# First attention: the rotation of q on VectorE, moved from between the maxima of slots 14 and 15 to ahead of the maximum of slot 14, behind the residual

## What is computed

```python
qkv = jnp.einsum('bsd,ed->bse', x, w_qkv)          # x: 32 x 256 x 128
q, k, v = jnp.split(qkv, 3, axis=-1)               # 16 heads of 8
q = _apply_rope(q, cos_emb, sin_emb)
k = _apply_rope(k, cos_emb, sin_emb)
scores = jnp.einsum('bhqd,bhkd->bhqk', q, k) / jnp.sqrt(8)
attn = jax.nn.softmax(scores, axis=-1)
out = jnp.einsum('bhqk,bhkd->bhqd', attn, v)
...
x = _layernorm(x + out @ w_out.T + b_out)
...
```

## Time and profile before

| | |
|---|---|
| median of 3 runs | 1514.56 us |
| lowest and highest run | 1513.92, 1516.4 us |
| profiled execution, its own time | 1516.91 us |
| profiled execution, span from first to last instruction | 1514.7 us |
| of the span: PE, PEld, DVE, ACT, POOL busy | 96%, 75%, 78%, 70%, 64% |
| loop of the first attention | about 60 to 460 us, 14.52 us a step |

### The profile page before, as it was taken

The page is one execution under the profiler, slowest core; times in us unless marked ns, Lnnn a source line. Parts: engine busy times, 40 slices in busy tenths (PEclk is TensorE's granted clock), DMA queues, the critical chain, the costliest instruction groups (busy, mean ns, idle before and its releaser), DMA issues. The chain is left out here.

```text
span 1514.7 us, 55309 instructions
## 1 busy us (share of the span) xinstructions
PE 1453.8 (96%) x17642; PEld 1143.0 (75%) x17642; DVE 1181.1 (78%) x3338; ACT 1057.0 (70%) x2581; POOL 966.3 (64%) x1160
## 2 busy tenths in 40 slices
PE   6999999999999899979999999999999999998998
PEld 4455555555554699959899999989998999997997
DVE  5788888888889388878778787878887888864666
ACT  2577777778778788847677777777777777773332
POOL 5555656656562277777777787788778877852222
PEclk9799999999999999979999999999999999999999
DMA  5454454545544001222322222222222222201111
GB/s 143 130 140 135 140 140 129 140 129 140 143 128 111 22 32 34 74 68 71 91 69 70 90 77 80 70 88 79 80 70 84 81 79 70 82 17 35 62 62 52
DMA packets 174124, 133.93 MB, mean 88 GB/s; under 512 B 13787, under 2 KB 145126, under 8 KB 174054
## 3 DMA queue, kind: packets, MB, share of 16 engines
q1 hardware_dynamic: 172512, 132.18, 30.0%
q10 hardware_dynamic: 1542, 0.86, 0.2%
HBM read 64.82 MB, written 55.05 MB: 79 GB/s over the span
## 5 line engine op out<-in xcount | busy, mean ns | idle before, releaser
L987 DVE TENSOR_REDUCE shifts<-bank 128x2 bf16<-128x512 f32 x1024 | 682.6, 687 | 143.5 <-PE bank L1133 142.8
L918 ACT ACTIVATE probs<-bank 128x512 f32<-128x512 f32 x1024 | 580.0, 596 | 111.7 <-PE bank L1119 105.8
L1081 PE MATMUL bank<-values,probs 64*128 64x129 f32 x8192 | 579.5, 277 | 0.9 <-DVE o_even L944 0.7
L1081 PEld LDWEIGHTS bank<-values,probs 64*128 64x128 f32 x8192 | 530.5, 189 | 20.3 <-issue 4.4
L1133 PE MATMUL bank<-stack 48*128 48x256 bf16 x2048 | 371.2, 276 | 21.4 <-DVE shifts L987 15.7
L1119 PE MATMUL bank<-stack 49*128 49x256 bf16 x2048 | 372.1, 274 | 8.1 <-ACT probs L918 2.7
L718 POOL TENSOR_TENSOR values<-mix,v_in 128x1024 f32<-128x1024 f32 x128 | 302.2, 2362 | 0.0
L1119 PEld LDWEIGHTS bank<-stack 49*128 49x128 bf16 x2048 | 163.9, 95 | 139.6 <-ACT probs L918 90.1
L727 POOL TENSOR_TENSOR o_odd<-o_odd,scaled 128x256 f32<-128x256 f32 x224 | 163.3, 729 | 131.4 <-ACT scaled L841 128.4
L841 ACT ACTIVATE scaled<-bank,recips 128x128 f32<-128x128 f32 x448 | 138.6, 360 | 93.3 <-DVE recips L971 93.2
L1133 PEld LDWEIGHTS bank<-stack 48*128 48x128 bf16 x2048 | 156.1, 96 | 43.6 <-DVE shifts L987 28.7
(11 more groups left out here) (165 smaller groups left out, 2177.7 us busy)
## 6 DMA issues: line engine op xcount, KB each, us to landing
stack<-score_parts SPq DMA_DIRECT2D x64, 512.0 KB, 4.2
stack<-score_parts SPq DMA_DIRECT2D x256, 96.0 KB
score_parts<-parts SPq DMA_DIRECT2D x253, 64.0 KB, 2.1
score_parts<-parts SPq DMA_DIRECT2D x128, 96.0 KB, 2.4
score_parts<-parts SPq DMA_DIRECT2D x64, 192.0 KB, 2.3
x_in_f<-x_all SPq DMA_DIRECT2D x64, 128.0 KB, 2.0
score_parts<-parts SPq DMA_DIRECT2D x64, 128.0 KB, 2.2
x_in<-in_L_attn_x SPq DMA_DIRECT2D x32, 128.0 KB, 2.2
```

The source lines that it names most:

```text
L918: act.activation(probs[:, s % RING, :, :].rearrange("p t n -> p (t n)"), s2[s % 2][:, :], ACT.Exp, scale=scale).then_inc(exp_done, 1)
L987: dve.tensor_reduce(shifts[:, :, hf, col], s1_bank(s)[:, :].rearrange("p (t n) -> p t n", t=TILES), op=ALU.max, axis=AX.X, negate=True).th ...
L1081: return pe.matmul(pv_bank(h)[:, q * (D + 1):(q + 1) * (D + 1)], probs[rows, h % RING, t, q * P:(q + 1) * P], values[b.odd][rows, t, h, :] ...
```

## The change

`rotate(i, 0, slots.q_ahead)` moves up by one maximum. Its condition changes from slot 15 (`slots.q + 1`) to slot 14 (`slots.q`), and it is written behind `add_residual` instead of ahead of it.

```diff
@@ step of VectorE
-                if first and s == slots.q + 1 and on(slots.q_ahead):
-                    rotate(i, 0, slots.q_ahead)
                 if first and s == slots.out and on(-1):
                     add_residual(i)
+                if first and s == slots.q and on(slots.q_ahead):
+                    rotate(i, 0, slots.q_ahead)
                 if on(1):
                     max_of_head(i.plus(1), s)
```

## The result

The kernel after takes 1504.1 us (median of 6 runs, 1501.08 to 1507.93) against 1514.33 us of the kernel before (6 runs, 1513.08 to 1516.4). The ratio is 0.993, with a 95% interval of 0.9919 to 0.9941: faster by 0.7%, 10.2 us. The forecast was 1504.1 us; that the two agree to 0.1 us is luck, since the interval allows a gain of 9 to 12 us.

The account below looks back on a forecast made before the run. TensorE bounds the kernel, losing 0.64 us a step to slot 15's maximum. 28 x 0.36 = 10.1 us plus 0.4 in the first step, together 10.5, takes the 1514.56 median to 1504.1 us; 8-in-10 range 1501.8 to 1509.4.

Parts of the forecast that it names:

- What bounds: First attention's loop: TensorE's first score of slot 1 waits for VectorE's maximum of slot 15, losing 0.64 us a step.
- The rotation's start: VectorE, behind the residual: the rotation starts 0.04 us after the q projection on TensorE, at 204.89.
- The maxima: VectorE, slots 14 and 15: they follow the rotation at 0.60 us intervals; slot 15's comes 0.36 us earlier, slot 14's 0.24 later.
- TensorE and what is late next: Loop step: slot 1's first score comes 0.36 us earlier; other engines and transfers wait for TensorE or have room.
- The sum: Whole kernel: 28 steps of 0.36 us give 10.1 us, with 0.4 in the first step 10.5 us.
- the term of 0.4: First step with maxima: rotation 0.54 us earlier, taken as 0.4 us because TensorE runs partly on the lower clock.
- The sign that everything behind the loop would look as before: From the second layer's start on, everything should look as before, 10 us earlier.
- The forecast's own range: Whole kernel: 1502.5 to 1506.5 us, from the delay's bounds, the first step and the runs' spread; forecast's chance 75%.
- part of the gain goes back to ScalarE: Slot 1: its exponential sets what follows, so only 0.19 us a step is won, 1509.2 us; 9%.
- nothing is won: Loop: a chain across steps sets 14.52 us a step and TensorE waits for a transfer instead, 1514.5 us; 8%.
- the chain over several steps: Loop: rotation to GpSimd to SyncE to stacked scores would set 14.52 us a step; part of an 8% rival.
- it becomes slower through the rotation's wait: Slots 14 and 15: a late projection signal delays rotation and maxima, 0.22 us a step, 1520.7 us; 4%.

Follow-up runs that it names:

- e6: Kernel after, with TensorE projecting q ahead of the output in slot 14 and the residual behind the maximum of slot 15: 1497.68 us, ratio 0.9898.
- e2: Kernel before, with the rotation moved ahead of slot 14's maximum in odd steps only: 1507.87 us, ratio 0.9959.
- e8: Kernel after, with TensorE projecting q behind the scores of slot 14 instead of ahead of them: 1521.38 us, ratio 1.0049.
- e3: Kernel before, with the residual moved behind the maximum of slot 15 and the rotation where it was: 1515.12 us, ratio 1.0.
- e4: Kernel after, with the residual moved behind the maximum of slot 15: 1503.56 us, ratio 0.9927.
- e5: Kernel after, with TensorE projecting q ahead of the output in slot 14 and VectorE rotating q ahead of the residual: 1503.83 us, ratio 0.9927.
- e1: Kernel after, with the rotation of q ahead of the residual as well: 1513.54 us, ratio 0.9986.
- e7: Kernel before, with TensorE projecting q behind the scores of slot 14 instead of ahead of them: 1506.56 us, ratio 0.9949.

## Why the prediction was right

*What bounds.* TensorE's wait at slot 1, 0.64 us a step by starts of instructions, was the right place and the right size. e6 takes nearly all of it, and the step shortens by as much.

*The rotation's start.* Forecast 0.04 us behind the projection, measured 0.04 us (200.59 to 200.63), as in the earlier trace rows. The Trainium skill ("Perfetto Trace Analysis", section "Tensor Engine Instruction (MATMUL, LD_WEIGHTS)") warns that the semaphore comes behind the modelled end. The runs agree, in that there is a delay, and put it at 0.04 us here. The section gives no figure, and the row of the same pair of instructions at the kernel's start gave the right one.

*The maxima.* Forecast to start 0.60 and 1.20 us behind the rotation; the two end at 202.52, 1.89 us behind its start, as 204.89 to 206.78 in the forecast. Slot 14's maximum came later and cost nothing.

*TensorE and what is late next.* The step was forecast at 14.16 us and is 14.16, with 0.28 us of loss left, as forecast. ScalarE was to keep waiting for TensorE; it does, with 0.18 us ahead of the turned maxima. Of transfers, TensorE's weight loads show one wait in the whole stretch (53 to 446 us), of 0.4 us; in e6, whose step is 0.60 us shorter than before, TensorE shows one between 100 and 400 us, of 0.2 us. So no transfer sets the step.

*The sum.* 28 x 0.36 = 10.1 us behind the first step, and 0.4 in it. In the traces the 26 steps from the first maximum of slot 15 with a residual ahead of it (76.27 before, 74.85 after) to the last with a rotation give 9.2 us (0.355 each), and the two steps ahead of these 0.61 and 0.36 us, the 0.61 beside a granted clock of 0.74 over 16 us instead of 0.69. What comes before cannot be told apart cleanly: the first maximum starts at 31.74 instead of 33.21 us, ahead of anything that the change touches, and the first two steps run partly on the lower clock. By the maximum of slot 15 of the first step the difference is 0.45 us, in the region of the 0.4 that I took, but with 1.5 us of other differences in front of it. Counted from the start of that step's q projection, TensorE's first score of slot 1 comes 4.06 us behind it instead of 4.60 (41.68 to 45.74 after, 41.60 to 46.20 before): 0.54 us, as much as the rotation could start earlier. How much of that the rest of the kernel keeps is not shown, so neither is the term of 0.4. The medians differ by 10.2 us against the 10.5 of the sum.

*Luck and what was off.* That the measured 1504.1 is the forecast to the last digit is luck: the sum was taken from a median of three runs that lay 0.2 us above that of all six, and the profiled execution, for which the same sum gave 1506.4 us, took 1507.93. The sign that everything behind the loop would look as before, 10 us earlier, held only to within the 1.6 us named above. The forecast's own range was also drawn a little tight: taken end to end, its terms give 1502.2 to 1507.1, not 1502.5 to 1506.5.

*The rivals.* That part of the gain goes back to ScalarE: not seen, its idle time in front of the turned maxima fell but stayed. That nothing is won: excluded by the measured gain, and the chain over several steps behind it by e2. That it becomes slower through the rotation's wait: not with the projection where it is, since its signal comes 0.04 us behind its end and not with the matmuls queued behind it. e8 shows what a late rotation costs, 0.51 us a step against e7, where 0.50 was expected; that e8 stands 0.21 us a step above the kernel before, close to the rival's 0.22, is chance, as its TensorE waits less at slot 1 than before.

## What to carry to other kernels

Where an in-order engine idles for one operand while another lies ready, the order of arrival on the producer should set the order of use: read both producers' ends from the timeline and put the work that is ready into the gap, and the work that fills a gap (here the residual) ahead of what still waits. Price such a move at the time by which the last instruction of the group starts earlier, not at the work that is moved: 0.33 us of work removed in e3 was worth nothing, and a swap with no work removed 0.36 us a step. Then look at the producer too: the next 0.24 us lay in the order of two projections on TensorE, together with the place of the residual. The residual's move alone (e4) won nothing, and the projections' order with the residual between rotation and maxima (e5) 0.03 us.

## What the runs showed of the hardware that I had not expected

- Counts of waits that are worked out in registers inside a loop can reach into the engine's time when the semaphore ahead of them arrives shortly before the engine is free: in e5 the residual followed the rotation by 0.61, 0.66 or 0.70 us, with no register instruction, one of 65 ns or one of 105 ns behind a wait that was met 0.16 us before VectorE was free. In e1, where the semaphore had been there for long, nothing was lost (0.61 us).
- A written-out step took less time than a loop step, in the kernel before 14.28 against 14.52 us and in the kernel after 13.93 against 14.16. Why is not shown.
- With bf16 scores between two groups of fp32 matmuls TensorE took 0.34 us more (2.40 us in e7 and e8 against 2.06 us before for the same matmuls), of which a wait for an exponential may be a part.
- The part of an execution behind the change moved by 1.6 us between two profiles, 0.6 us of it beside a lower granted clock of TensorE (0.89 against 0.90 over 120 us), while a step of the loop repeated to 0.01 us.
